# Macaron block: expert 0's first three row blocks turned on TensorE, the other experts' slot positions worked out inside the experts' loop, and expert 0's weight splits made to wait for a count of issued gathers

## The reference

```python
x = x + 0.5 * ffn(layernorm(x))
x = x + attention(layernorm(x))
x = x + 0.5 * ffn(layernorm(x))

def ffn(x):                      # N = 8192 rows, D = 256, 8 experts, F = 1024
    logits = xf @ router_w.T
    topw, topi = top_k(softmax(logits), 2)
    # each expert keeps the 1280 (= capacity) rows of largest weight
    disp[e, pos] = xf[rows of expert e]
    g, u = disp @ wg, disp @ wu
    eo = (silu(g) * u) @ wd
    out[row] += eo * weight
```

## Time and profile before

| | us |
|---|---|
| median of 3 runs | 1842.58 |
| lowest and highest run | 1841.14, 1844.77 |
| the profiled execution, its own time | 1838.82 |
| span of its trace, first to last instruction | 1837.1 |
| PE busy in it | 1613.4 (88%) |
| DVE busy | 1165.4 (63%) |
| ACT busy | 896.1 (49%) |
| POOL busy | 783.1 (43%) |

### The profile page before, as it was taken

The page is one execution under the profiler, slowest core; times in us unless marked ns, Lnnn a source line. Parts: engine busy times, 40 slices in busy tenths (PEclk is TensorE's granted clock), DMA queues, the critical chain, the costliest instruction groups (busy, mean ns, idle before and its releaser), DMA issues.

```text
span 1837.1 us, 40742 instructions
## 1 busy us (share of the span) xinstructions
PE 1613.4 (88%) x14463; PEld 1248.0 (68%) x14463; DVE 1165.4 (63%) x2841; ACT 896.1 (49%) x1627; POOL 783.1 (43%) x608
## 2 busy tenths in 40 slices
PE   4647999999999999976899774699999999999997
PEld 3535777777777777763677663467777787777776
DVE  8898574838475665526898897745463746456451
ACT  5634454545445454525666464345453545445452
POOL 6503526152434435036776550333525163544513
PEclk9999999999999999996899765799999999999999
DMA  7754426061614334036666451434425161624412
GB/s 224 254 167 127 74 83 129 26 132 38 140 41 114 62 93 78 9 44 168 151 142 148 135 199 37 128 62 95 74 82 127 28 135 44 132 52 103 75 12 30
DMA packets 277752, 183.41 MB, mean 100 GB/s; under 512 B 177450, under 2 KB 264372, under 8 KB 277684
## 3 DMA queue, kind: packets, MB, share of 16 engines
q1 hardware_dynamic: 246964, 139.90, 27.9%
q0 software_dynamic: 30720, 42.62, 14.6%
HBM read 89.66 MB, written 55.05 MB: 79 GB/s over the span
## 4 chain that ended last, share of the span: by engine, by line
PE 73%; DVE 10%; issue 6%; ACT 3%; POOL 3%; DMA 2%; another core or an unknown queue 1%; SPq 1%; DVEq 0%; POOLq 0%; ACTq 0%
PE bank L1531 45%; PE bank L1543 23%; POOL rstd L446 1%; PE bank L1482 1%; PE bank L1513 1%; POOL rows L450 1%; DVE gat L1307 1%; ACT xn L799 1%; DVE v L1301 1%; PE bank L1575 1%; DMA xs<-in_L_attn_x 1%; DVE xn L1056 1%; SPq L578 1%; PE bank L1607 1%
## 5 line engine op out<-in xcount | busy, mean ns | idle before, releaser
L1531 PE MATMUL bank<-xT,w_g 128*128 128x320 f16 x3072 | 502.1, 299 | 23.5 <-DMA xT<-gat 23.5
L1531 PE MATMUL bank<-xT,w_u 128*128 128x320 f16 x3072 | 502.4, 300 | 0.3 <-DVE unit_buf L1171 0.3
L1171 DVE SCALAR_TENSOR_TENSOR unit_buf<-bank,sc_cur,unit_buf 128x320 f32<-128x320 f32 x512 | 281.8, 550 | 333.2 <-PE bank L1531 245.8
L1543 PE MATMUL bank<-w_d,xs 128*128 128x256 f16 x3840 | 439.9, 275 | 26.7 <-issue 19.8
L741 ACT ACTIVATE unit_buf<-bank,sc_cur 128x320 f32<-128x320 f32 x512 | 270.0, 527 | 357.0 <-PE bank L1531 346.4
L1543 PEld LDWEIGHTS bank<-w_d,xs 128*128 128x128 f16 x3840 | 376.8, 99 | 85.6 <-issue 29.8
L1531 PEld LDWEIGHTS bank<-xT,w_g 128*128 128x128 f16 x3072 | 292.1, 98 | 132.3 <-issue 23.7
L1531 PEld LDWEIGHTS bank<-xT,w_u 128*128 128x128 f16 x3072 | 301.1, 98 | 118.3 <-DVE unit_buf L1171 0.7
L423 POOL DMA_INDIRECT gat<-rows_d,id_next x160 | 185.5, 1159 | 314.3 <-issue 169.1
L416 POOL TENSOR_TENSOR hot_v<-hot_b,val 128x160 bf16<-128x160 bf16 x112 | 93.5, 835 | 392.8 <-DVE hot_b L1150 392.8
L1177 DVE TENSOR_TENSOR xs<-unit_buf,xs 128x320 f16<-128x320 f32 x512 | 247.0, 482 | 2.2
(11 more groups left out here) (231 smaller groups left out, 1691.5 us busy)
## 6 DMA issues: line engine op xcount, KB each, us to landing
rows_d<-rows SPq DMA_DIRECT2D x32, 512.0 KB, 3.4
raw_gu<-in_L_ffn_wg SPq DMA_DIRECT2D x16, 1024.0 KB
raw_gu<-in_L_ffn_wu SPq DMA_DIRECT2D x16, 1024.0 KB
raw_d<-in_L_ffn_wd SPq DMA_DIRECT2D x16, 1024.0 KB, 5.2
x_d<-xs SPq DMA_DIRECT2D x1, 8192.0 KB, 33.0
out_x<-xs SPq DMA_DIRECT2D x16, 512.0 KB, 3.4
xs<-in_L_attn_x SPq DMA_DIRECT2D x7, 1024.0 KB, 5.7
xs<-x_d SPq DMA_DIRECT2D x5, 1024.0 KB, 5.7
```

Source lines behind the costliest of these rows:

```text
L1171: dve.scalar_tensor_tensor(h32[:, u % HB, :], bank[2 + u % 2][:, 0:CW], sc_cur[:, 4:5], act_s[:, u % 2, :], mult, mult).then_inc(S.h32_rea ...
L1531: mm = pe.matmul(bank[2 * m + u % 2][:, 0:CW], wgu[m][:, w, k, f * P:(f + 1) * P], xT[:, a * KD + k, c * CW:(c + 1) * CW], start=(j == 0 a ...
L1543: mm = pe.matmul(bank[4 + s % 2][:, 0:D], hid[:, a, f, s * P:(s + 1) * P], wdn[:, w, f, :], start=(f == 0 and j == 0), stop=(f == FT - 1 a ...
```

## The change

There are five edits.

1. `PARTS` becomes (0, 1), (2), (3, 4), (5, 6, 7), (8, 9).
2. For expert 0 of each stage, SP leaves out the transposes of blocks 0, 1 and 2. PE makes four 128x128 transposes of each of these blocks into banks 7, 4 and 2, behind the eight list pieces, and ACT copies each bank to `xT`.
3. `positions` for experts 1 to 7 leaves the stretch behind `list_read`. It is called in the experts' loop behind unit 0, for one expert at a time, and reads the slots from `t3` (called `slots`), to which ACT has copied `bank[5]`.
4. POOL increments `first_rows_issued` behind the third gather in its program. DVE waits for it ahead of the second of expert 0's four splits.
5. `back_turned` is renamed `turned_by_pe` and counts the new transposes too.

```diff
-    PARTS = ((0,), (1, 2), (3, 4), (5, 6, 7), (8, 9))
+    PARTS = ((0, 1), (2,), (3, 4), (5, 6, 7), (8, 9))
+    AHEAD = 3
...
+        AHEAD_BANK = (7, 4, 2)
+        slots = t3
...
                             bounds_check=N - 1).then_inc(gathered[j], 16)
+                        if first and s == AHEAD - 1:
+                            pool.sem_inc(first_issued, 1)
...
                 for j, blocks in enumerate(PARTS):
+                    if units is None and blocks[-1] < AHEAD:
+                        continue
...
                 for k in range(4):
                     split_hi(k % 2, k // 2, S.gu_hi)
+                act.wait_ge(S.hot_b_ready, 1)
+                act.activation(slots[:, :, :].rearrange("p t e -> p (t e)"), bank[5][:, :], ACT.Copy).then_inc(S.slots_ready, 1)
+                for s in range(AHEAD):
+                    act.wait_ge(S.turned_by_pe, s + 2)
+                    act.activation(xT[:, :, s * P:(s + 1) * P],
+                                   bank16[AHEAD_BANK[s]][:, 0:2 * D].rearrange("p (c n) -> p c n", n=P),
+                                   ACT.Copy).then_inc(turned[0], 16)
...
+            def positions(ch, n, slots_of):
+
+                slot, p = col(slots_of, n)[:, 0], col(pos_b, n)[:, 0]
+                ch.step(dve.tensor_scalar(pos_i[:, :], slot, 1.0 / P, ROUND, mult, add))
+                ch.step(dve.tensor_scalar(p, pos_i[:, :], ROUND, float(P), sub, mult))
                 for twin in range(2):
...
+                    ch.mark(dve.scalar_tensor_tensor(col(pos_a, n)[:, 0, :, twin], slot, HALF, p, add, sub))
                 ch.wait()
...
                     if last:
                         continue
+                    if u == 0:
+                        positions(ch, n, slots[:, :, :].rearrange("p t e -> p e t"))
...
                 list_read(S, ch, 0)
-                positions(ch, 1, E - 1)
                 for k in range(4):
+                    if k == 1:
+                        dve.wait_ge(first_issued, S.scaled + 1)
                     dve.wait_ge(S.gu_hi, k + 1)
                     split_lo(k % 2, k // 2, S.gu_lo)
+                dve.wait_ge(S.slots_ready, 2)
...
+                for s in range(AHEAD):
+                    if s in (0, AHEAD - 1):
+                        pe.wait_ge(gathered[s // 2], 16 * len(PARTS[s // 2]) * (S.first + 1))
+                    for c in range(2 * KD):
+                        i = pe.transpose(bank16[AHEAD_BANK[s]][:, c * P:(c + 1) * P], gat[:, s, c * P:(c + 1) * P],
+                                         ident16[:, :])
+                    i.then_inc(S.turned_by_pe, 1)
                 with pe.Fori(0, E - 1) as e:
```

More of the change, by code:

```diff
@@ L257, in macaron_block @@
         turned = [sem(f"rows_turned{c}") for c in range(CH)]
+        first_issued = sem("first_rows_issued")
         sems = [ffn_sems("a"), ffn_sems("b")]
@@ L416, in list_piece, with gather @@
                 pool.tensor_tensor(hot_v[:, r], bc(hot_b[:, r], 2, 2), bc(val[:, at, :], 3, ST), mult).then_inc(S.hot_v_ready, 1)
-            def gather(S, n):
+            def gather(S, n, first=False):
                 pool.wait_ge(S.ids_ready, n + 1)
@@ L471, in ffn @@
                     pool.wait_ge(stored, 16 + 16 * STEPS + (16 * G4 if stored is S.stored0 else 0))
-                gather(S, 0)
+                gather(S, 0, True)
                 pool.wait_ge(S.kept, 16 * (1 if S is sems[0] else B * QUADS))
@@ L1129, in route @@
                 weight_scales(S, ch, 0)
[L1131 to L1139 removed]
+                dve.wait_ge(S.turned_by_pe, 1)
+                positions(ch, 0, bank[5][:, :].rearrange("p (t e) -> p e t", e=E))
+            def positions(ch, n, slots_of):
+                slot, p = col(slots_of, n)[:, 0], col(pos_b, n)[:, 0]
+                ch.step(dve.tensor_scalar(pos_i[:, :], slot, 1.0 / P, ROUND, mult, add))
+                ch.step(dve.tensor_scalar(p, pos_i[:, :], ROUND, float(P), sub, mult))
                 for twin in range(2):
[L1141 to L1142 removed]
+                    ch.mark(dve.scalar_tensor_tensor(col(pos_a, n)[:, 0, :, twin], slot, HALF, p, add, sub))
                 ch.wait()
@@ L1506, in route @@
                     last = pe.transpose(back[:, g], rT[:, g * P:(g + 1) * P], ident[:, :])
-                last.then_inc(S.back_turned, 1)
+                last.then_inc(S.turned_by_pe, 1)
             def list_piece(S, n, i):
```

13 lines of the change are left out of this document (2 added, 11 removed).

## The result

| us | before | after |
|---|---|---|
| median of 8 runs each | 1842.74 | 1850.61 |
| lowest and highest | 1839.83, 1844.77 | 1843.48, 1855.89 |
| the profiled execution | 1838.82 | 1850.53 |
| its span | 1837.1 | 1848.8 |
| ACT waits for a block of the down projection, released by "remote" | 8, 37.5 us | 17, 74.5 us |

A forecast was written before the change was run, and what follows sets the result against it. PE's 23.5 us of waiting for expert 0's `xT` transposes, in both stages, was the ceiling. First stage +0.3, second -0.85, loop 0 gave -0.55 us: 1842.0 us against the median of 1842.58, range 1837.5 to 1846.0.

The forecast's parts named there:

- the gaps of the down projection: PE's 26.7 us idle in the down projections may shift by 4 us either way: 1838.6 or 1846.6 us; chance 0.16.
- Transposes on PE: Expert 0, each stage: tail from gather 2's end to PE is 3.6 instead of 6.3 us, 2.7 earlier with gather 2 on time.
- The hold that doesn't hold: Expert 0's splits on DVE: POOL's sequencer raises the count about 1.7 us after its first move, while gather 0 still runs.
- A gather waits for the end of the split beside it: Expert 0: splits delay gathers 1 and 2, so gather 2 ends 1.4 us late in A, 1.8 in B.
- second rival: Both stages gain in full, as gathers and expert 1's raw weights land sooner: 1837.2 us; chance 0.08.
- the first: Rival: DVE's wait holds as written, or gathers aren't slowed; B gains 2.7 us, total 1840.2 us; chance 0.15.
- The second stage: Expert 0 of B: PE starts at 1165.8 us, 0.85 us earlier, counted as -0.85 us.
- The first stage: A: PE's 1.3 us earlier start is lost waiting for DVE, held by expert 1's raw weights; load later, +0.3 us.
- The clock: PE starts expert 0 at 1.2 GHz; how long it stays there is open, 1 us either way allowed in B.
- Positions in the loop: Four small DVE instructions behind unit 0, about 1.2 us, fit in 1.53 us of slack: cost 0.

The follow-up runs named there:

- e11: Changed kernel without the gathers of experts 1 to 7 in the first stage and without SP's transposes of them in the second; down projections 214.6 and 232.5 us.
- e13: Changed kernel with gathers 5 to 9 of experts 1 to 7 spread between the scatters; 1796.76 us beside 1848.81 for the kernel before, ratio 0.9700.
- e15: Changed kernel with the loop's gathers spread and DVE's hold on the landing of expert 0's third gather; 1792.13 us beside 1849.50 for the kernel before, 0.9690.
- e6: Changed kernel with DVE's hold on the landing of expert 0's third gather; 1841.19 us beside 1840.48 for the kernel before, ratio 1.0002.
- e2: Kernel before with the new transpose groups alone; 1797.01 us beside 1796.35 for the kernel before, ratio 1.0001.
- e5: Kernel before with twelve more identity transposes on PE ahead of the experts' loop; 1796.27 us beside 1796.35 for the kernel before, ratio 1.0003.
- e9: Kernel before with the new transpose groups alone, run again on another chip; 1796.88 us beside 1798.06 for the kernel before, ratio 0.9994.
- e14: Kernel before with gathers 5 to 9 of experts 1 to 7 spread between the scatters; 1799.01 us beside 1849.50 for the kernel before, ratio 0.9728.
- a2: Changed kernel as it is, on a chip without late signals; 1794.01 us beside 1797.90 for the kernel before, ratio 0.9978.
- e1: Changed kernel with the transpose groups of before; 1795.38 us beside 1796.35 for the kernel before, ratio 0.9993.
- e8: Changed kernel with the transpose groups of before, run again on another chip; 1793.70 us beside 1798.06 for the kernel before, ratio 0.9983.
- e10: Changed kernel with the transpose groups of before, beside the changed kernel on one chip; 1795.51 us against 1797.90 for the kernel before, ratio 0.9989.

## Why the prediction was wrong, step by step

**The term that failed is the gaps of the down projection.** The prediction saw 26.7 us there, "mostly for its own issue", gave them no cause, and let them shift by 4 us either way, with a chance of 0.16. In the profiled executions that term was +11.0 us, idle time and clock together. The idle time alone is 0 to 35.9 us, by chip and kernel. What the runs show in its place: the term comes from the ten gathers in a row of the loop, and goes when they are left out (e11) or the last five are spread (e13 to e15); without late signals the change gains 3.9 us. Which part of the change made the term larger on the other chips stays open. The view of waits of before had the lead that was not followed: ACT, "remote", 37.5 us in 8 waits, all for blocks of the down projection. PE's idle time put down to "issue" and ACT's waits put down to "remote" stood in the same down projections and went away together.

**Transposes on PE: right.** Where PE's matmuls hang on the rows, the tail from the end of gather 2 to PE was worked out as 3.6 us and measured 148.69 - 145.28 = 3.41; in the second stage it was 3.43.

**The hold that doesn't hold: right.** DVE's second split began at 140.72, 0.9 us behind the start of gather 0 (forecast near 140, with gather 0 where it was before). In the second stage it waited 1.08 us.

**A gather waits for the end of the split beside it: right.** Forecast for gathers 1 and 2 in the first stage were waits of 0.4 and 1.1 us; they came out as 0.44 and 1.07 us, and PE's start at 8.88 us behind gather 0 instead of 9.0. Moving the splits away (e6) removed both delays. The splits take 1.28 us either way.

The Trainium skill, page "SBUF — State Buffer", section "Who interferes with whom", infers that a DVE instruction with two SBUF inputs doesn't hold up the writing of descriptors. The same gathers at 2.08 us beside splits and at 1.01 without them say otherwise. Its rule that a DVE instruction with two SBUF inputs contends with a GpSimd instruction that reads SBUF agrees with them, if the gather counts as one. (The sum that the prediction says the inference shares with its second rival, 2.7 us in the second stage alone, is that of the first.)

**The second stage: direction right, size low.** Forecast was 0.85 us, the start came 1.19 us earlier. From gather 0 to the last matmul of the stage it is 650.9 to 651.3 us in the four kernels without late blocks whose blocks SP turns (e2, e5, e9, e14), and 648.8 to 649.4 in the five with PE's transposes and the hold as written (a2, e1, e8, e10, e13): 2.0 us less on average.

**The first stage: part of the gain was kept, and the reason given was wrong.** The same stretch of the first stage is 653.6 to 654.9 us in the four and 653.2 to 653.6 in the five: 0.7 us less on average, where 0.3 us more was forecast. So the two stages together gain 2.8 us, which agrees with the 3.9 us (2.3 to 5.6) of a2. The forecast let PE stand 1.7 us for DVE at unit 10, behind DVE's wait for the raw weights, and that did not come. DVE's wait fell, from 2.28 to 1.54 us, and PE did not stand there:

```profile
167.09 0.69 DVE L931 TENSOR_REDUCE am<-raw_gu 128x1 f32<-128x512 f32 x1 [1.54 <-DMA raw_gu<-in_L_ffn_wg]
```

The raw weights landed 27.3 us behind gather 0, against 28.4 before: 1.2 us earlier in this pair and 0.15 in another (a2 against e14), where the forecast had them 0.3 us later.

**The clock: it differs from run to run.** In the second stage PE worked at the low level for 3.2 us behind its first unit's start before and for 5.8 us now. One window of that stage, before and then after (columns: window, its length, busy time of PE, PE's weight loads, DVE, ACT, POOL, granted clock, DMA share, GB/s):

```profile
1170.00:1172.00 2.00, 2.00 (x17) 1.46 (x15) 0.71 (x2) 1.13 (x3) 1.01 (x1) 1.00 0.33 82
```

```profile
1170.00:1172.00 2.00, 2.00 (x9) 1.11 (x8) 0.00 (x0) 0.53 (x1) 1.45 (x2) 0.50 0.68 175
```

It is 17 matmuls at 2.4 GHz, 3.3 us behind the first unit's start, and then 9 at 1.2 GHz, 1.4 us behind it. But one kernel differs from itself by as much. The groups alone have 5.5 us at the low level in the first stage of e2 and 2.7 in that of e9, and the changed kernel has 5.8, 3.3, 3.2 and 2.8 us in the second stage of its four profiles. So this pair says nothing of the change. The 1 us either way allowed in the second stage is about what such a difference of 2 to 3 us at half the speed costs; in the first it was allowed nothing, since PE was to stand for DVE there.

**Positions in the loop: right, they cost nothing.** The units of experts 1 to 6 take 53.93 us in every kernel, and in the first stage of expert 1 the four instructions end inside DVE's slack:

```profile
239.51 0.21 DVE L1152 TENSOR_SCALAR pos_i<-t 128x64 f32 x1
...
240.22 0.45 DVE L1155 SCALAR_TENSOR_TENSOR pos_a<-t,pos_b  x2 [0.16 <-DVE pos_b L1153]
240.96 0.55 DVE L1184 SCALAR_TENSOR_TENSOR unit_buf<-bank,sc_cur,unit_buf 128x320 f32<-128x320 f32 x1 [0.29 <-DVE pos_a L1155]
```

## What to carry to other kernels

Idle time with no releaser but "issue" is a cause that hasn't been found, not noise: if it is many times the gain at stake, find what runs beside it (here ten gathers in a row) before costing the edit, and try to move that work. A hold on another engine should wait for a landing: a count raised behind an indirect DMA in POOL's program rises before that transfer has been worked on. And a loss of a few us should be measured on more than one chip, since here its sign depended on which. The same goes for one pair of traces: PE's time at the low clock behind an idle stretch differed by 2.8 us between two profiles of one kernel.

## What was not expected of the hardware

- The kernel before takes 1796 to 1798 us on three chips and 1840 to 1850 us on five.
- On four of the five (on the fifth, chip 7, no kernel with the ten gathers in a row was profiled), with gathers issued 1.3 to 1.6 us apart, ACT and DVE saw PE's results late, by 4.2 us in the block worked out above, and PE stood still, 27 to 36 us in all. With the last five 3.3 us and more apart no block of the down projection was late, and the kernel took 3% less.
- Most of that idle time of PE, 24.9 of 31.4 us in the changed kernel, stood in the middle of a block, where its program waits for nothing.
- A gather on POOL that comes up beside a split on DVE waits for that split's end: 1.01 us alone, up to 2.09 beside a split. The split takes 1.28 us either way.
